# One mask matmul per unit, and the split transposed rows kept in DRAM for the second pass of self-attention

## The chip, the cores and the metric

The kernel runs on 1 core of one Trainium2 chip. The metric is device time in microseconds of one execution of the whole program: self-attention, cross-attention and a mixture of experts. A core has a matrix engine (TensorE, "PE" in the profile, with its weight loads as "PEld"), a vector engine (DVE), a scalar engine (ACT), GpSimd (POOL) and a sync engine (SP) which here only issues transfers; 16 DMA engines move data between DRAM and the on-chip memory SBUF. Each engine works through its own list of instructions in order, and engines wait for one another through semaphores.

## The reference

The change touches the first of three residual blocks:

```python
x = x + attn(layernorm(x))        # B=16, S=256, H=512
x = x + xattn(layernorm(x), ctx)  # untouched
x = x + experts(layernorm(x))     # untouched

# attn: 16 heads of 128, 4 key/value groups
q = (x @ w_q)                      # 512 -> 2048
k, v = split(x @ w_kv)             # 512 -> 4*128 each
scores = q @ k.T / sqrt(128);  scores[key > query] = -inf
probs = softmax(scores);  out = (probs @ v) @ w_dense
```

## The kernel before

Tokens are handled in *pairs*: two sequences, 512 tokens. There are 8 pairs (`PAIRS`), and they are run through twice (`HALVES`): the weights of all 16 heads don't fit in SBUF, so the first pass computes 8 heads, the second the other 8 and adds to the rows that the first pass stored. The loop variable `t` runs from 0 to 15; it is written as a loop over t = 0 to 6 (kind "plain"), t = 7 ("turn", where the next half's weights are loaded), t = 8 ("fresh"), a loop over t = 9 to 14 ("plain" again) and t = 15 ("last").

Precision is kept by splitting every float32 operand into a high part (an fp32r copy made by ACT) and a low part (the remainder, made by DVE). `product3` (L513) multiplies such pairs in three matmuls: high·high and the two mixed ones.

For each t the normalised rows are needed transposed and split, as `xT` (two tiles, 1 MB each). To make them for t+1, during pair t: SP loads the rows into `x_in` (L210); DVE computes `row_stats` in units 3 to 6 (L366), `mean_and_variance` in unit 7, `apply_norm` in units 9 to 12 (L376), with a power on POOL between them; PE transposes 16 blocks of 128 x 128 in units 14 and 15 (`xT_fill`, L531, eight in each); ACT and DVE split them (L336, L361). Both passes do this, from the same rows.

A pair then consists of 16 *units* u = 0 to 15, a unit being one head of one sequence. In unit u PE does, in this order: `scores(u)`; half a projection of a later query (`q_fill`, u up to 11); in odd units `values_product`, the product of probabilities and values for two earlier units; the transposes of the probabilities of unit u-1 (L591); in units 14 and 15 `xT_fill`; in units 12 to 15 a quarter of `dense`, the output projection. After unit 15 comes a tail: `k_fill` and `v_fill` of t+1, the rest of `dense`, two query projections and `scores(t+1, 0)`.

`scores` (L563) fills a PSUM bank in two blocks: queries 0 to 127 against 128 keys, and queries 128 to 255 against 256 keys. Each block is three split matmuls and then a bf16 matmul of the identity with a triangular block of -1e30 (L575, `causal`) which masks the diagonal 128 columns. The softmax of a unit follows on other engines: DVE takes two maxima (L404, L405), ACT two exponentials (L294, L296), DVE the inverse sums and the first third of the scaling (L412, L414), POOL the rest of the scaling (L260), then PE transposes the result (L591), ACT and DVE split that (L289, L361), and `values_product` uses it. On DVE, unit u is: maxima(u), the step of the normalisation if there is one, the inverse (u), in odd units the low parts of a query and of a context, and the low part of the transposed probabilities of u-1 (`pT_low_part`).

SP issues everything in one queue, in order: rows `x_in`, residual rows `acc`, and the store of `acc` at the end of a pair, each behind a wait.

Of the kernel before, what the change touches and what calls it, by code (L numbers as in the profile page):

```python
# [20 lines left out]
P = 128  # L21
BANK = 512
# [11 lines left out]

def attention_phase(nc, x_rows, w_q, w_kv, w_dense, x1_rows, TOKENS, HIDDEN, SEQ, HEADS, GROUPS):

# [17 lines left out]
    with ExitStack() as ctx:  # L54
# [6 lines left out]
        def sem(name):  # L61
            return ctx.enter_context(nc.semaphore("a_" + name))
# [48 lines left out]
        rstd_done = sem("rstd_done")  # L111
        xn_done = sem("xn_done")
        proj_filled = sem("proj_filled")
        proj_high = sem("proj_high")
# [24 lines left out]
        def heads_context(c, n):  # L139

            m, b = unit(2 * n)
            return c[:, m // HPG, m % HPG:m % HPG + 2, b * SEQ:(b + 1) * SEQ]

        def tokens(rows, pair):
# [46 lines left out]
        with nc.Block() as block:  # L191
            @block.sync
            def _(sp):
# [12 lines left out]
                def body(t, kind, half):  # L206
                    if kind != "last":
                        wait_alone(sp, xn_done, TB * (t + 1), (consts, 6))
                        nxt = 0 if kind == "turn" else t + 1 - half * PAIRS
                        sp.dma_start(x_in[:], tokens(x_rows, nxt)).then_inc(x_loaded, 16)  # L210
                    if kind == "fresh":
                        load_weights(1, DENSE)
                    if kind == "turn":
                        sp.wait_ge(proj_filled, FILLS * t + KT + G + 2)
                        load_weights(1, KV)
                    wait_alone(sp, stored, 16 * (t + 1), (consts, 6))
                    rows = x_rows if half == 0 else x1_rows
                    sp.dma_start(acc[:], tokens(rows, t - half * PAIRS)).then_inc(acc_loaded, 16)
                    if kind == "turn":
                        sp.wait_ge(proj_filled, FILLS * (t + 1))  # L220
                        load_weights(1, QUERY)
                    if kind != "last":
                        wait_alone(sp, d_added, G * TB * (t + 1) + 1, (consts, 6))
                        sp.dma_start(tokens(x1_rows, t - half * PAIRS), acc[:]).then_inc(stored, 16)
                    else:
                        for n in range(TB):
                            sp.wait_ge(d_added, TB * (G * t + G - 1) + n + 1 + 1)
                            sp.dma_start(tokens(x1_rows, t - half * PAIRS)[:, n, :], acc[:, n, :]).then_inc(stored, 16)
# [5 lines left out]
            def _(pool):  # L234
# [21 lines left out]
                def body(t, kind, half):  # L256
                    for u in range(UNITS):
                        s = u % 2
                        wait_alone(pool, rinv_done, UNITS * t + u + 1, (consts, 6))
                        nc.gpsimd.tensor_scalar(probs[:, s, P:3 * P], probs[:, s, P:3 * P], rinv[:, s, 1:2], None,  # L260
                                                ALU.mult).then_inc(probs_done, 1)
                        if u == TB + 3 and kind != "last":
                            norm_scale(t + 1)
# [4 lines left out]
            def _(act):  # L268
# [53 lines left out]
                def body(t, kind, half):  # L322
                    last = kind == "last"
                    for u in range(UNITS):
# [6 lines left out]
                        if u >= 1:  # L331
                            probs_transposed(t, u - 1)
                        if u in XT_STEPS and not last:
                            for j in range(*XT_STEPS[u]):
# [24 lines left out]
            def _(dve):  # L359
# [98 lines left out]
                def body(t, kind, half):  # L458
                    last = kind == "last"
                    for u in range(UNITS):  # L460
                        if u:
                            maxima(t, u)
                        if not last:

# [12 lines left out]
                        if u >= 1:  # L477
                            pT_low_part(t, u - 1)
                        if not last:
                            if u in XT_STEPS:  # L480
                                xT_low(t + 1, *XT_STEPS[u])
                        if kind == "turn" and u in SPLIT_AT_TURN[1]:
# [29 lines left out]
            def _(pe):  # L512
# [50 lines left out]
                def scores(t, u):  # L563
# [5 lines left out]
                    for qb in range(2):  # L569
                        c0, n = qb * P, (qb + 1) * P  # L570
                        q0 = b * SEQ + qb * P
                        product3(ps_s[s][:, c0:c0 + n], qT, (slice(None), m % 4, slice(q0, q0 + P)),
                                 kT, (slice(None), g, slice(b * SEQ, b * SEQ + n)), True, False)

                        ins = nc.tensor.matmul(ps_s[s][:, c0 + n - P:c0 + n], ident_b[:], causal[:], start=False, stop=True)  # L575
                    ins.then_inc(s_filled, 1)

# [58 lines left out]
                def body(t, kind, half):  # L636
                    last = kind == "last"
                    for u in range(UNITS):
# [7 lines left out]
                        if u >= 1:  # L646
                            transposes(t, u - 1)
                        if u in XT_STEPS and not last:
                            xT_fill(t + 1, *XT_STEPS[u])
                        if u == UNITS - 4:  # L650
                            pe.wait_ge(w_low, NCH * (half + 1))
# [3 lines left out]
                    if kind == "turn":  # L655
                        pe.wait_ge(w_low, NCH + KV[-1] + 1)
                    if not last:
                        k_fill(t + 1, 0)
# [1672 lines left out]
def decoder_layer(nc, x, context, mask, mask_cols, a_wq, a_wkv, a_wd, x_wq, x_bq, x_wk, x_bk, x_wv, x_bv,  # L2331
# [11 lines left out]

    attention_phase(nc, by_512(x), a_wq, a_wkv, a_wd, by_512(x1), B * S, H, S, HEADS, GROUPS)
    cross_attention_phase(nc, x1, context, mask, mask_cols, x_wq, x_bq, x_wk, x_bk, x_wv, x_bv, aux, rinv, x2)
# [45 lines left out]
```

## Time and profile before

| | |
|---|---|
| median of 3 runs (range) | 3019.73 us (3019.2 to 3022.58) |
| the profiled execution's own time | 3024.8 us |
| its span, first to last instruction | 3023.3 us |
| PE busy | 2648.8 us, 88% of the span |
| DVE busy | 1931.0 us (64%) |
| ACT busy | 1352.9 us (45%) |
| POOL busy | 1040.0 us (34%) |

Self-attention is the first part of the span, until 1392 us, when its last store is issued. In it the granted TensorE clock is full. A row of a timeline tells when an instruction started, how long it took, engine, source line, operation and operands, and in brackets how long the engine had been idle before it and for whom. Durations of matmuls include the time in the pipeline, so the distance between the *starts* of successive matmuls tells what one costs, not its duration.

### The profile page before, as it was taken

Reading aid. Unit: us, or ns where it says so; the run is one execution under the profiler, and the core shown is the slowest. Engines: PE = TensorE matmul, PEld = TensorE weight load, DVE = VectorE, ACT = ScalarE, POOL = GpSimd, SP = SyncE. Lnnn points to the kernel's source line nnn. Section 1 sums busy time; section 2 is a strip of 40 time slices with the busy share of each in tenths; the row PEclk is TensorE's granted clock in tenths of the full one; section 3 lists DMA queues with packets and bytes.
Section 4 is the critical chain, followed back from the end, with each engine's and each line's share of the span. In section 5 each row is a group of like instructions: output and inputs, shape, how many; then the busy total and the mean of one; then the engine's idle time right before and its main releaser. Section 6 shows DMA issues by size and latency. Waiting matters only on the chain. (4 is left out here: it accounts for less than half of the span.)

```text
span 3023.3 us, 49992 instructions
## 1 busy us (share of the span) xinstructions
PE 2648.8 (88%) x15042; PEld 1814.2 (60%) x15043; DVE 1931.0 (64%) x3971; ACT 1352.9 (45%) x2725; POOL 1040.0 (34%) x1209
## 2 busy tenths in 40 slices
PE   7999999999999999995788889888888434299997
PEld 6888888888888888884333333333333111166665
DVE  6555566656555666554888878888888278444443
ACT  4333444444333444432477766776666322022221
POOL 2111122211111222213355565566555346432322
PEclk9999999999999999997899999999999666599999
DMA  3110011122110111103666777777776264455554
GB/s 112 42 42 28 13 42 42 42 84 70 43 42 0 42 42 42 42 28 88 113 121 135 140 128 130 133 137 131 132 138 114 54 230 158 157 98 104 98 104 77
DMA packets 140545, 265.50 MB, mean 88 GB/s; under 512 B 39217, under 2 KB 42161, under 8 KB 138945
## 3 DMA queue, kind: packets, MB, share of 16 engines
q1 hardware_dynamic: 111376, 195.58, 29.1%
q0 software_dynamic: 24496, 60.72, 9.7%
q10 hardware_dynamic: 4608, 8.39, 0.8%
q8 instruction: 34, 0.56, 0.1%
q14 instruction: 31, 0.25, 0.0%
HBM read 139.43 MB, written 64.90 MB: 68 GB/s over the span
## 5 line engine op out<-in xcount | busy, mean ns | idle before, releaser
L1420 DVE TENSOR_REDUCE b_negmax<-b_ps_s 128x2 f32<-128x1024 f32 x512 | 616.8, 1221 | 117.6 <-PE b_ps_s L1563 114.2
L1292 ACT ACTIVATE b_probs<-b_ps_s 128x1024 f32<-128x1024 f32 x512 | 517.1, 1022 | 258.3 <-PE b_ps_s L1574 257.2
L260 POOL TENSOR_SCALAR probs<-probs,rinv 128x256 f32<-128x256 f32 x256 | 242.2, 946 | 1099.7 <-DVE rinv L412 1099.7
L294 ACT ACTIVATE probs<-ps_s,negmax 128x128 f32<-128x128 f32 x256 | 94.2, 368 | 480.6 <-DVE negmax L405 480.6
L1563 PE MATMUL b_ps_s<-b_stack 54*128 54x512 f32 x1024 | 228.8, 444 | 80.0 <-ACT b_probs L1292 50.1
L1574 PE MATMUL b_ps_s<-b_stack 56*128 56x512 f32 x1024 | 255.1, 496 | 49.4 <-DVE b_negmax L1420 30.8
L1574 PEld LDWEIGHTS b_ps_s<-b_stack 56*128 56x128 f32 x1024 | 97.9, 189 | 333.6 <-issue 183.9
L1585 PE MATMUL b_ps_o<-b_probs,b_v_stack 128*32 128x512 f32 x2048 | 283.6, 627 | 5.2 <-ACT b_probs L1292 5.2
L516 PE MATMUL ps_proj<-xT_h,wq_h 128*128 128x512 f32 x512 | 215.6, 421 | 0.0
L2181 POOL DMA_INDIRECT out<-e_y,e_place_int x71 | 110.8, 1560 | 277.1 <-DVE e_y L2244 174.7
L516 PE MATMUL ps_proj<-xT_h,wq_l 128*128 128x512 f32 x512 | 201.2, 393 | 0.0
L516 PE MATMUL ps_proj<-xT_l,wq_h 128*128 128x512 f32 x512 | 199.9, 390 | 0.0
L1563 PEld LDWEIGHTS b_ps_s<-b_stack 54*128 54x128 f32 x1024 | 101.2, 193 | 138.0 <-ACT b_probs L1292 79.5
L1171 POOL TENSOR_TENSOR b_out_tiles<-b_o_sb,b_out_tiles 128x512 f32<-128x512 f32 x64 | 82.5, 1290 | 263.1 <-DMA b_out_tiles<-row_sum_inverses 263.1
L516 PE MATMUL ps_s<-kT_h,qT_h 128*128 128x128 f32 (+1 forms) x512 | 164.3, 321 | 0.0
L516 PE MATMUL ps_d<-wd_h,cT_h 128*128 128x512 f32 x384 | 158.0, 412 | 1.4 <-DVE cT_l L361 1.4
L412 DVE RECIPROCAL rinv<-rowsum 128x2 f32<-128x2 f32 x256 | 42.3, 165 | 178.9 <-ACT probs L296 178.9
L2318 PE MATMUL e_ps_h<-c_w_h,e_xT_l 128*128 x284 | 152.5, 537 | 0.0
L516 PE MATMUL ps_d<-wd_h,cT_l 128*128 128x512 f32 x384 | 151.0, 393 | 0.0
L516 PE MATMUL ps_d<-wd_l,cT_h 128*128 128x512 f32 x384 | 150.6, 392 | 0.0
L361 DVE TENSOR_TENSOR pT_l<-ps_pT,pT_h 128x384 fp32r<-128x384 f32 x256 | 140.8, 550 | 2.6 <-ACT pT_h L289 2.6
L516 PE MATMUL ps_s<-kT_l,qT_h 128*128 128x128 f32 (+1 forms) x512 | 142.4, 278 | 0.0
(299 smaller groups left out, 6730.1 us busy)
## 6 DMA issues: line engine op xcount, KB each, us to landing
b_stack<-b_split SPq DMA_DIRECT2D x240, 128.0 KB
e_row<-rows_by_expert SPq DMA_DIRECT2D x71, 258.0 KB, 3.2
x_in<-in_x SPq DMA_DIRECT2D x16, 1024.0 KB, 7.5
b_out_tiles<-row_sum_inverses SPq DMA_DIRECT2D x64, 256.0 KB
x<-acc SPq DMA_DIRECT2D x15, 1024.0 KB, 5.1
b_stack<-b_late SPq DMA_DIRECT2D x96, 128.0 KB
acc<-in_x SPq DMA_DIRECT2D x8, 1024.0 KB, 6.0
acc<-x SPq DMA_DIRECT2D x8, 1024.0 KB, 5.7
```

The lines of the kernel that those rows point to most:

```text
L260: nc.gpsimd.tensor_scalar(probs[:, s, P:3 * P], probs[:, s, P:3 * P], rinv[:, s, 1:2], None, ALU.mult).then_inc(probs_done, 1)
L294: nc.scalar.activation(probs[:, s, 0:P], ps_s[s][:, 0:P], ACT.Exp, bias=negmax[:, s, 0:1], accum_out=rowsum[:, s, 0:1])
L361: return nc.vector.tensor_tensor(dst, ps, h.bitcast(F32), ALU.subtract)
L516: ins = nc.tensor.matmul(out, w[a][w_at], m[b][m_at], start=st, stop=en)
L1171: nc.gpsimd.tensor_tensor(r_b[:, q, :], o_sb[:, q, :], r_b[:, q, :], ALU.mult).then_inc(o_scaled, 1)
L1292: nc.scalar.activation(probs[:, k % 2, p, :, :], ps[:], ACT.Exp, scale=0.25).then_inc(e_done, 1)
L1420: nc.vector.tensor_reduce(negmax[:, k, p, :], ps[:], AX.X, ALU.max, negate=True).then_inc(m_reduced, 1)
L1563: ins = nc.tensor.matmul(ps[:, i, :], stack[rows, quad, 0, p, k * P:(k + 1) * P], stack[rows, quad, 1, p, :], start=True, stop=True)
L1574: ins = nc.tensor.matmul(ps[:, i, :], stack[rows, q, 1, p, k * P:(k + 1) * P], stack[rows, q, 0, p, :], start=True, stop=True)
L1585: ins = nc.tensor.matmul(ps_o[32 * h:32 * h + 32, :], v_stack[:, k, HQ * q + h, :], probs[:, k % 2, h // 2, h % 2, :], start=(k == 0), sto ...
L2181: nc.gpsimd.indirect_dma_start(out, bass.IndirectOffsetOnAxis(place_int[i][:], 0), y[i][:], None, compute_op=ALU.add).then_inc(y_out[i], 16)
L2318: ins = nc.tensor.matmul(ps_h[i][:], xT[a][:, i, j, :], w13[c][:, bass.ds(e, 1), j, :].rearrange("p o f -> p (o f)"), start=(m == 0), stop ...
```

## The change

There are two edits.

**The mask.** Instead of one bf16 matmul of 128 columns behind each of the two blocks, one matmul behind both adds the mask to the two diagonal blocks (columns 0 to 127 and 256 to 383) by strided and repeated access patterns. The flag that opens an accumulation is set only for the first block.

**The transposed rows.** A DRAM tensor `normalised_x_split` (16 MB) keeps `xT` of every pair. In the first pass SP stores both tiles; in the second pass, and for its first pair already in t = 7, SP loads them back once the last query projection of pair t has read the old ones. For these eight (t+1 = 8 to 15) the row load, the statistics, the normalisation, the 16 transposes and the splits are gone; what keeps the semaphore counts right are plain increments in unit 15. `k_fill` of t+1 now waits for the loads. The first pass is otherwise as it was.

```diff
+        def given(kind, half):
+            return kind == "turn" or half == 1 and kind != "last"
+        def made(kind, half):
+            return kind == "plain" and half == 0
 # SP
-                    if kind != "last":
+                    if kind == "plain" and half == 0:
                         wait_alone(sp, xn_done, TB * (t + 1), (consts, 6))
-                        nxt = 0 if kind == "turn" else t + 1 - half * PAIRS
-                        sp.dma_start(x_in[:], tokens(x_rows, nxt)).then_inc(x_loaded, 16)
+                        sp.dma_start(x_in[:], tokens(x_rows, t + 1)).then_inc(x_loaded, 16)
+                    if half == 0:
+                        wait_alone(sp, proj_low, FILLS * t + KT, (consts, 6))
+                        for i in range(2):
+                            sp.dma_start(xT_pairs[t, i], xT[i][:].bitcast(F32)).then_inc(xT_stored, 16)
...
                     if kind == "turn":
-                        sp.wait_ge(proj_filled, FILLS * (t + 1))
+                        sp.wait_ge(xT_stored, 32 * PAIRS)
+                    if given(kind, half):
+                        wait_alone(sp, proj_filled, FILLS * (t + 1), (consts, 6))
+                        for i in range(2):
+                            sp.dma_start(xT[i][:].bitcast(F32), xT_pairs[t + 1 - PAIRS, i]).then_inc(xT_loaded, 16)
+                    if kind == "turn":
                         load_weights(1, QUERY)
 # ACT (DVE and PE have the same pattern)
-                        if u in XT_STEPS and not last:
+                        if u == UNITS - 1 and given(kind, half):
+                            act.wait_ge(proj_filled, FILLS * (t + 1) + KT)
+                            act.sem_inc(proj_high, KT)
+                        if u in XT_STEPS and made(kind, half):
+                            if u == UNITS - 2:
+                                act.wait_ge(xT_stored, 32 * (t + 1))
 # DVE
-                        if not last:
+                        if made(kind, half):
                             if 3 <= u < 3 + TB:
                                 row_stats(t + 1, u - 3)
 # PE
                         product3(ps_s[s][:, c0:c0 + n], qT, (slice(None), m % 4, slice(q0, q0 + P)),
-                                 kT, (slice(None), g, slice(b * SEQ, b * SEQ + n)), True, False)
-                        ins = nc.tensor.matmul(ps_s[s][:, c0 + n - P:c0 + n], ident_b[:], causal[:], start=False, stop=True)
-                    ins.then_inc(s_filled, 1)
+                                 kT, (slice(None), g, slice(b * SEQ, b * SEQ + n)), qb == 0, False)
+                    diagonal = ps_s[s][:].rearrange("p (c k) -> p c k", c=BANK // P)[:, 0:3:2, :]
+                    nc.tensor.matmul(diagonal, ident_b[:], causal[:, None, :].to_broadcast([P, 2, P]),
+                                     start=False, stop=True).then_inc(s_filled, 1)
...
+                    if given(kind, half):
+                        pe.wait_ge(xT_loaded, 32 * (t + 2 - PAIRS))
                     if not last:
                         k_fill(t + 1, 0)
```

Where this puts the instructions can be seen in three places. On PE, unit 14 of a pair in the second pass's loop, before (`ps_s` is the bank of scores, `ps_pT` the transposed probabilities, `ps_proj<-ident,xn` the transposes of the normalised rows; the last two rows come a second time behind these, for the other bank, and then `dense`):

```order
L516 MATMUL ps_s<-kT_h,qT_l 128x128
L575 MATMUL ps_s<-causal,ident_b 128x128
L516 MATMUL ps_s<-kT_h,qT_h 128x256
L516 MATMUL ps_s<-kT_l,qT_h 128x256
L516 MATMUL ps_s<-kT_h,qT_l 128x256
L575 MATMUL ps_s<-causal,ident_b 128x128
L591 MATMUL ps_pT<-ident,probs 128x128 [waits a_probs_done,a_probs_done_first]
L591 MATMUL ps_pT<-ident,probs 128x128 x2
L527 ISA
L523 ISA [waits a_xn_done]
L531 MATMUL ps_proj<-ident,xn 128x128 [waits a_proj_low]
L531 MATMUL ps_proj<-ident,xn 128x128 x3
```

The same place on PE in the changed kernel, whose line numbers are higher:

```order
L543 MATMUL ps_s<-kT_h,qT_l 128x128
L543 MATMUL ps_s<-kT_h,qT_h 128x256
L543 MATMUL ps_s<-kT_l,qT_h 128x256
L543 MATMUL ps_s<-kT_h,qT_l 128x256
L603 MATMUL ps_s<-causal,ident_b 128x2x128
L619 MATMUL ps_pT<-ident,probs 128x128 [waits a_probs_done,a_probs_done_first]
L619 MATMUL ps_pT<-ident,probs 128x128 x2
L643 REGISTER_ALU
L543 MATMUL ps_d<-wd_h,cT_h 128x512 [waits a_d_added]
```

The first mask matmul is gone, the second covers both blocks, and the eight transposes of this unit (and eight in unit 15) have left PE. In the first pass the scores are the same as here, and the transposes stay.

On SP, the second pass's loop over t = 9 to 14, before:

```order
L210 ISA [waits a_xn_done,a_consts]
L210 DMA x_in<-in_x 128x4x512
L30 REGISTER_ALU
L218 ISA [waits a_stored,a_consts]
L218 DMA acc<-x 128x4x512
L30 ISA
L224 DMA x<-acc 128x4x512 [waits a_d_added,a_consts]
```

And the same loop on SP in the changed kernel:

```order
L231 ISA [waits a_stored,a_consts]
L231 DMA acc<-x 128x4x512
L237 ISA [waits a_proj_filled,a_consts]
L237 DMA xT_h<-normalised_x_split 128x2048
L237 ISA
L237 DMA xT_l<-normalised_x_split 128x2048
L30 ISA
L242 DMA x<-acc 128x4x512 [waits a_d_added,a_consts]
```

The 1 MB row load at the start of the pair is gone, and two loads of 1 MB stand behind the last query projection, in unit 11.

On PE, the end of unit 15 and the head of the tail in the changed kernel, second pass, where the wait for these loads stands (`a_xT_loaded`):

```order
L619 MATMUL ps_pT<-ident,probs 128x128 [waits a_probs_done,a_probs_done_first]
L619 MATMUL ps_pT<-ident,probs 128x128 x2
L689 ISA
L563 REGISTER_ALU [waits a_xT_loaded]
L550 REGISTER_ALU [waits a_proj_low]
L543 MATMUL ps_proj<-xT_h,wkv_h 128x512 [waits a_proj_low]
```

The first product of the tail is the first instruction that reads the loaded tiles.

## Rows read from the trace of the kernel before

**Rows 1.** Busy time by windows, 40 us of a second-pass pair; columns PE, PEld, DVE, ACT, POOL, granted clock, DMA share, GB/s

```profile
1065.00:1105.00 40.00, 40.00 (x251) 34.88 (x250) 29.09 (x83) 21.40 (x71) 11.64 (x13) 1.00 0.24 79
```

**Rows 2.** Waits in the first 1400 us; columns total us, times, longest us

```profile
DVE negmax L404 <- PE ps_s L575: 22.5, 15, 1.5
...
DVE stats L366 <- DMA x_in<-in_x: 18.4, 15, 7.0
...
PE ps_c L516 <- DVE pT_l L361: 4.6, 5, 1.8
...
PE ps_pT L591 <- POOL probs L260: 2.9, 8, 1.1
```

**Rows 3.** Timeline of PE, unit 11 of pair t = 12; columns start us, us

```profile
1098.11 0.27 PE L516 MATMUL ps_s<-kT_h,qT_l 128*128 128x128 f32 x1
...
1098.46 0.28 PE L516 MATMUL ps_s<-kT_l,qT_h 128*128 128x256 f32 x1
1098.58 0.28 PE L516 MATMUL ps_s<-kT_h,qT_l 128*128 128x256 f32 x1
1098.70 0.23 PE L575 MATMUL ps_s<-causal,ident_b 128*128 128x128 bf16 x1
...
1099.06 0.39 PE L516 MATMUL ps_proj<-xT_l,wq_h 128*128 128x512 f32 x1
1099.29 0.40 PE L516 MATMUL ps_proj<-xT_h,wq_l 128*128 128x512 f32 x1
```

**Rows 4.** Timeline of PE, first scores of units 14 and 15, pairs t = 11 and 15

```profile
1025.81 0.22 PE L516 MATMUL ps_s<-kT_h,qT_h 128*128 128x128 f32 x1
...
1030.60 0.22 PE L516 MATMUL ps_s<-kT_h,qT_h 128*128 128x128 f32 x1
...
1365.38 0.22 PE L516 MATMUL ps_s<-kT_h,qT_h 128*128 128x128 f32 x1
...
1369.32 0.22 PE L516 MATMUL ps_s<-kT_h,qT_h 128*128 128x128 f32 x1
```

**Rows 5.** Timeline of DVE, maxima of units 9 and 11, t = 7, and between

```profile
663.82 0.28 DVE L404 TENSOR_REDUCE negmax<-ps_s 128x1 f32<-128x128 f32 x1
...
665.42 0.17 DVE L412 RECIPROCAL rinv<-rowsum 128x2 f32<-128x2 f32 x1 [0.53 <-ACT probs L296]
...
670.05 0.28 DVE L404 TENSOR_REDUCE negmax<-ps_s 128x1 f32<-128x128 f32 x1
```

**Rows 6.** Timeline of DVE, maxima of units 1 and 11, pair t = 12

```profile
1068.77 0.29 DVE L404 TENSOR_REDUCE negmax<-ps_s 128x1 f32<-128x128 f32 x1 [1.50 <-PE ps_s L575]
...
1099.38 0.28 DVE L404 TENSOR_REDUCE negmax<-ps_s 128x1 f32<-128x128 f32 x1
```

**Rows 7.** Timeline of PE, transposes of the probabilities of unit 11, t = 12

```profile
1102.42 0.50 PE L591 MATMUL ps_pT<-ident,probs 128*128 128x128 f32 x3
```

**Rows 8.** Timeline of PE, first score of unit 0, pairs t = 9, 12, 13, 15

```profile
805.00 0.22 PE L516 MATMUL ps_s<-kT_h,qT_h 128*128 128x128 f32 x1
...
1060.02 0.22 PE L516 MATMUL ps_s<-kT_h,qT_h 128*128 128x128 f32 x1
...
1144.72 0.22 PE L516 MATMUL ps_s<-kT_h,qT_h 128*128 128x128 f32 x1
...
1314.87 0.22 PE L516 MATMUL ps_s<-kT_h,qT_h 128*128 128x128 f32 x1
```

**Rows 9.** Timeline of the DMA issues of SP, behind unit 11's query projection, t = 7

```profile
669.67 0.88 SPq L199 DMA_DIRECT2D wq_raw<-in_a_wq  x2
```

**Rows 10.** Timeline of PE, first matmul of the tail of t = 7

```profile
692.13 0.48 PE L516 MATMUL ps_proj<-xT_h,wkv_h 128*128 128x512 f32 x1
```

**Rows 11.** DMA issues, 668 to 690 us; columns KB each, median us to landing

```profile
wq_raw<-in_a_wq SPq DMA_DIRECT2D x2, 1024.0 KB, 7.1
```

**Rows 12.** DMA issues, whole trace, then 722 to 745 us (start of t = 8)

```profile
x_in<-in_x SPq DMA_DIRECT2D x16, 1024.0 KB, 7.5
...
x_in<-in_x SPq DMA_DIRECT2D x1, 1024.0 KB, 7.6
```

More of the change, by code:

```diff
@@ L32, in wait_alone, with attention_phase @@
     eng.wait_ge(sem, value)
-def attention_phase(nc, x_rows, w_q, w_kv, w_dense, x1_rows, TOKENS, HIDDEN, SEQ, HEADS, GROUPS):
+def attention_phase(nc, x_rows, w_q, w_kv, w_dense, xT_pairs, x1_rows, TOKENS, HIDDEN, SEQ, HEADS, GROUPS):
     D = P
@@ L112, in attention_phase @@
         xn_done = sem("xn_done")
+        xT_stored = sem("xT_stored")
+        xT_loaded = sem("xT_loaded")
         proj_filled = sem("proj_filled")
@@ L261, in body @@
                                                 ALU.mult).then_inc(probs_done, 1)
-                        if u == TB + 3 and kind != "last":
+                        if u == TB + 3 and made(kind, half):
                             norm_scale(t + 1)
@@ L478, in body @@
                             pT_low_part(t, u - 1)
-                        if not last:
-                            if u in XT_STEPS:
-                                xT_low(t + 1, *XT_STEPS[u])
+                        if made(kind, half) and u in XT_STEPS:
+                            if u == UNITS - 2:
+                                dve.wait_ge(xT_stored, 32 * (t + 1))
+                            xT_low(t + 1, *XT_STEPS[u])
+                        if u == UNITS - 1 and given(kind, half):
+                            dve.wait_ge(proj_high, FILLS * (t + 1) + KT)
+                            dve.sem_inc(proj_low, KT)
                         if kind == "turn" and u in SPLIT_AT_TURN[1]:
@@ L647, in body @@
                             transposes(t, u - 1)
-                        if u in XT_STEPS and not last:
+                        if u in XT_STEPS and made(kind, half):
                             xT_fill(t + 1, *XT_STEPS[u])
+                        if u == UNITS - 1 and given(kind, half):
+                            pe.wait_ge(proj_low, FILLS * (t + 1))
+                            pe.sem_inc(proj_filled, KT)
                         if u == UNITS - 4:
@@ L2342, in by_512 @@
         return t.rearrange("(g b) s h -> g (b s) h", b=BANK // S)
-    attention_phase(nc, by_512(x), a_wq, a_wkv, a_wd, by_512(x1), B * S, H, S, HEADS, GROUPS)
+    xT_pairs = nc.dram_tensor("normalised_x_split", [B * S // BANK, 2, P, H // P, BANK], F32, kind="Internal").ap()
+    attention_phase(nc, by_512(x), a_wq, a_wkv, a_wd, xT_pairs, by_512(x1), B * S, H, S, HEADS, GROUPS)
     cross_attention_phase(nc, x1, context, mask, mask_cols, x_wq, x_bq, x_wk, x_bk, x_wv, x_bv, aux, rinv, x2)
```

## The prediction, made before the changed kernel ran

> **What bounds the kernel now.** I read the busy time by windows first, then the list of waits, then timelines of single pairs. The window shows PE busy for all of its 40 us, at full clock, and DVE for 29 [rows 1]: by busy time the phase is PE's, and everything taken off PE is gained. The waits say it more sharply. In the first 1400 us PE waits 4.6 us for DVE and 2.9 us for POOL. But DVE, which takes 256 maxima, waits for PE's scores only 15 times, once per pair, in unit 1 [rows 2, 6]. An engine that never waits for PE in units 2 to 12 is as slow as PE there. So I looked at its pace.
>
> DVE's maxima of units 9 and 11 start 6.23 us apart [rows 5]. Within, DVE waits for ACT's exponentials even behind a normalisation step (0.53 us idle before the inverse [rows 5]): that step lies in ACT's shadow, and taking it away only makes the idle longer. DVE and PE meet in the softmax of unit 11: its transposes stand behind the scores of unit 12 without a query projection between, so there PE meets DVE's result. In t = 12 the maxima of unit 1 start at 1068.77, those of unit 11 at 1099.38 (30.61 us), and the transposes start 3.04 us later, behind the inverse and POOL's scaling [rows 6, 7]. The row of these transposes has no wait in brackets: PE's own work took the same 33.65 us, so the two are level. PE can get faster, but those 33.65 us stay, a floor that DVE, ACT and POOL set from unit 1 to the transposes in unit 12. Outside (units 13, 14, 15, the tail, units 0 and 1) DVE waits for PE.
>
> **The mask.** A matmul's price is the distance of starts. From the last 128-column split matmul to the second 256-column one are 0.35 us, with the mask and one 256-column matmul between; the unmasked steps would be 0.12 + 0.12 (the step from 1098.46 to 1098.58), so the mask costs 0.11 to 0.12. From the last 256-column one to the second projection matmul are 0.48 us, of which 0.12 and 0.23 are theirs: 0.13 [rows 3]. A mask of 128 columns thus costs as much as a 256-column matmul (0.12). So I take it that a mask of 256 columns costs the same 0.12 to 0.13, and one of two vanishes: 0.12 us per unit. The bounds: the longer stream adds what half a 256-column matmul does, 0.06, and only 0.06 is saved; or the changed weights between 128- and 256-column groups cost nothing extra, and 0.13 is.
>
> The rule against this is in the Trainium skill, "TensorE: Matmul & The Clock Gate", section "Step-by-step: what each phase is for": the array takes in one column per cycle, so a stream costs its columns alone. By it two masks of 128 and one of 256 cost the same and this edit gives 0. Its figure for 128 columns is 55.6 ns; the trace disagrees, with 110 to 130 ns for these, so I follow the trace and keep the rule as a rival.
>
> There are 256 units, but the gain counts only where PE is the later one. Scores(2) to scores(12), 11 of 16, lie inside the floor. If PE gets ahead by 11 x 0.12 = 1.3 us there, it waits 1.3 us for POOL before the transposes of unit 11, or earlier for DVE before a `values_product`. Five per pair are left (units 13, 14, 15, 0, 1): 80 x 0.12 = **9.6 us** (4.8 at 0.06, 10.4 at 0.13).
>
> **The transposes.** Unit 14 takes 4.79 us in t = 11, with eight transposes, and 3.94 us in t = 15, which makes none [rows 4]: 0.85 us for eight, 1.70 for 16. Units 14 and 15 lie outside the floor. Nothing else comes to bind: t = 15 runs the same DVE adds and softmax, and PE had no wait in its 3.94. Eight pairs (t = 7 to 14) lose them: 8 x 1.70 = **13.6 us** (12.8 if the transposes of unit 15 were partly hidden, 14.4 if ACT's and DVE's splits held something back).
>
> **Statistics, normalisation, splits** on DVE, ACT and POOL: 0, since DVE's pace does not come from them. But the row load is waited for, 18.4 us in 15 times, one of them 7.0 at the start [rows 2], and that wait, in unit 3, is longer than ACT's shadow in some pairs and lengthens the floor. The six pairs t = 9 to 14 take (1314.87 - 805.00) / 6 = 84.98 us on average; t = 12 takes 84.70 [rows 8]. Without a row load all should be like t = 12: 6 x 0.28 = 1.7, and some 0.3 for t = 7 and 8: **2.0 us**. In the first pass the wait stays, and scores(1) now end 0.12 earlier than the unmoved landing of the rows: -0.4 us for seven pairs.
>
> **The loads.** In t = 7 SP issues two loads of 1 MB behind unit 11's query projection, at 669.67, exactly where the new loads go; they land 7.1 us after issue [rows 9, 11]. The first reader of `xT`, the tail's first matmul, starts at 692.13 [rows 10], 22.5 us after. Less the 1.7 us of transposes that leaves 20.8: the loads are hidden with over 12 us to spare. Nothing is queued behind the wait for `proj_filled` on SP but the store at the pair's end. In t = 7 the 2 MB of query weights move behind the new 2 MB; at the same rate they land by about 14 to 15 us after issue, and their first reader on ACT stands in unit 15. Cost 0.
>
> **The stores.** In the first pass 2 MB go out behind the row load and before `acc`. Does that delay the rows, which DVE waits for? At t = 8 two 1 MB weight loads are issued right behind the rows, and the rows land after 7.6 us [rows 12], against a median of 7.5 over all 16. What is queued behind does not delay. `acc` comes later by up to 6 us and is not read before unit 12. The tiles are overwritten in unit 14, over 50 us later. Cost 0, at most the 0.5 us by which loads differ, in seven pairs: 3.5.
>
> **The sum.** 9.6 + 13.6 + 2.0 - 0.4 = 24.8 us off the profiled execution's 3024.8, which is 3000.0. Its median is 5.1 us lower, and nothing here depends on that: 3019.7 - 24.8 = **2994.9**, say 2995. Edges from the bounds: 4.8 + 12.8 + 0 - 0.4 - 3.5 = 13.7 off (3006); 10.4 + 14.4 + 2.5 = 27.3 off (2992). The later phases stay as they are, at the same clock.
>
> **The rivals.**
> *The floor does not hold.* If DVE's chain follows PE (its lag behind the scores is nearly constant within a pair, as a follower's would be), all 256 masks count: 256 x 0.12 = 30.7, and with 13.6 + 2.0 that is 46 off: 2973. Against it: DVE is idle in units 2 to 12 only for ACT, never for scores. 8%.
>
> *The merged mask saves nothing.* Its columns cost in full, or the strided output and the repeated input cost as much as a second matmul. Then 13.6 + 1.6 = 15.2 off: 3004.5. For it stands the column count; against it the 0.12 us for 128 columns. 13%. The rule of the Trainium skill named above gives this case.
>
> *The loads come too late.* One mechanism: `k_fill` of eight tails waits for `xT_loaded`. It starts to cost when 2 MB take over 20.8 us, and turns the whole into a loss when they take 3.1 us more (24.8 / 8), 24 us, against 7.1 measured; at 28 us it would be 8 x 7.2 - 24.8 = +33, or 3053. For it: in no trace were fp32r tiles written by 8 KB rows during units 11 to 15. Against it: three times the time. 4%.
>
> That the change does not do what it says can be left out for the transposes, which leave the list of PE.
>
> **Chances.** Forecast 72%, floor broken 8%, mask free of gain 13%, loads late 4%, and 3% for something that I don't see. The range of 80% goes from 2984 to 3007: it takes in the forecast's own 2992 to 3006 and the useless mask, with some room below for a floor that gives way in part, and leaves out the broken floor and the late loads. A measurement here tells 0.2%, 6 us, from nothing. Faster by more: the first three cases, 92%. Within: 4%, for a useless mask together with a small cost of the stores. Slower: 4%.
>
> **What would show it.** PE should have 256 mask matmuls of 256 columns and 128 fewer transposes. Units 14 and 15 of t = 7 to 14 should be shorter by 0.85 + 0.12 each; t = 9 to 14 should take 84.7 - 1.7 - 0.6 = 82.4 us each, all alike, and pairs of the first pass 84.2 to 84.9 instead of 84.8 to 85.5. PE's waits for POOL before the probabilities' transposes and for DVE before `values_product` should grow from 7.5 us to about 7.5 + 16 x 1.2 = 27 us: that is where the other 11 masks go. From the maxima of unit 1 to the transposes of unit 11 it should still be 33.6 us. If that stretch is 32.3, the floor was none. If the distance of starts across the merged mask is 0.18 or more, the mask term is too large. A wait of PE for a transfer ahead of the tail would show the late loads, and waits for rows in the first pass over 1.4 us a cost of the stores.

## The result and the profile after

The changed kernel takes 3005.2 us in the median of five runs (3002.5 to 3010.2), the kernel before 3019.7 (five runs, 3016.9 to 3025.1). The ratio is 0.9948, with a 95% interval from 0.9932 to 0.9964: 14.5 us less (10.9 to 20.5). The forecast was 24.8 less. The direction is right, the time lies inside the range, and some ten microseconds of the gain are missing. The measured 3005.2 is nearer to 3004.5, the figure of the rival in which the merged mask saves nothing, than to the forecast's 2994.9. The time alone would speak for that rival; it takes the traces and the experiments to tell them apart.

The page of the changed kernel (busy time, share of the span, instructions) shows that the work did go:

```profile
span 3008.7 us, 49088 instructions
...
PE 2619.4 (87%) x14658; PEld 1775.2 (59%) x14659; DVE 1879.3 (62%) x3843; ACT 1331.9 (44%) x2693; POOL 1029.5 (34%) x1193
```

The groups of PE by line and form in the first 1400 us (busy us, mean ns, idle before) have one mask per unit, 256 columns wide, and half of the 256 transposes of the normalised rows:

```profile
L603 PE MATMUL ps_s<-causal,ident_b 128*128 128x256 bf16 x256 | 72.9, 285 | 0.0
...
L558 PE MATMUL ps_proj<-ident,xn 128*128 128x128 f32 x128 | 18.4, 292 | 14.2 <-DVE xn L399 13.3 <-DVE xT_l L384 0.8
```

**Where the time came from.** The first scores of unit 0 in pairs t = 1, 7, 9 and 15, on PE's timeline (start us, us); the answer to [rows 8]:

```profile
117.79 0.22 PE L543 MATMUL ps_s<-kT_h,qT_h 128*128 128x128 f32 x1
...
630.18 0.22 PE L543 MATMUL ps_s<-kT_h,qT_h 128*128 128x128 f32 x1
...
802.59 0.22 PE L543 MATMUL ps_s<-kT_h,qT_h 128*128 128x128 f32 x1
...
1298.22 0.22 PE L543 MATMUL ps_s<-kT_h,qT_h 128*128 128x128 f32 x1
```

The six pairs t = 9 to 14 take 1298.22 - 802.59 = 495.63 us, 82.6 each and all alike within 0.03; before they took 509.87 [rows 8]. That is 14.24 less. Pairs t = 7 and 8 give 4.4 more. The pairs of the first pass, however, became slower: t = 1 to 6 take 630.18 - 117.79 = 512.39 us, 85.40 each. Before they began at 118.00 and 628.21, 510.21 us or 85.04 each. Up to the start of t = 15 the changed kernel is 1314.87 - 1298.22 = 16.65 us ahead. The cross-attention begins 18.6 us earlier (its first row on DVE starts at 1376.59 instead of 1395.18).

From there to the end this one execution took 4.0 us more than the one of before. Nothing there was changed. Over eleven profiled executions of this case's kernels that stretch took between 1617.1 and 1636.7 us, so a difference of 4 between two of them tells nothing. I compare the attention by its landmarks and the whole by the medians.

**What is waited for.** The list of waits in the first 1400 us (total us, times, longest us), to be read beside [rows 2]:

```profile
DVE rinv L435 <- ACT probs L314: 217.6, 250, 1.5
...
DVE negmax L427 <- PE ps_s L603: 22.2, 15, 1.5
DVE stats L389 <- DMA x_in<-in_x: 15.9, 7, 6.7
...
PEld ps_c L543 <- issue: 12.2, 32, 1.0
PEld ps_pT L619 <- issue: 10.2, 22, 0.6
...
PE ps_c L543 <- DVE pT_l L384: 8.5, 11, 2.4
...
PE ps_pT L619 <- POOL probs L278: 5.9, 17, 0.4
```

The row of the kernel before that belongs to the first:

```profile
DVE rinv L412 <- ACT probs L296: 178.9, 242, 1.2
```

Three things stand in it. PE's two rows grew from 7.5 to 14.4 us, and the idle time of the weight loads for which the profile names nobody (the "issue" rows) from 4.6 to 22.4: PE now meets the softmax chain more often. DVE waits for rows only 7 times instead of 15, but still 15.9 us, instead of 18.4: without the 6.7 at the start, 1.5 us per wait where there were 0.8. And DVE, which lost half of its normalisation work, waits 39 us longer for ACT's exponentials: most of the work taken off it became idle time. No wait of PE for the loaded `xT` is in the list.

### The profile page after: what moved, and what is told of

Its sections match the earlier page's. It is cut to its first block and busy times, and to the rows that moved or that the text cites. A ratio compares the mean times of both kernels' runs of the same rounds, so it can differ in the third digit from the quotient of the medians.

```text
span 3008.7 us, 49088 instructions
## 1 busy us (share of the span) xinstructions
PE 2619.4 (87%) x14658; PEld 1775.2 (59%) x14659; DVE 1879.3 (62%) x3843; ACT 1331.9 (44%) x2693; POOL 1029.5 (34%) x1193
## 5 line engine op out<-in xcount | busy, mean ns | idle before, releaser
L543 PE MATMUL ps_s<-kT_h,qT_h 128*128 128x128 f32 (+1 forms) x512 | 156.7, 306 | 0.0
L543 PE MATMUL ps_s<-kT_h,qT_l 128*128 128x128 f32 (+1 forms) x512 | 142.2, 278 | 0.0
```

The source lines that it names most:

```text
L543: ins = nc.tensor.matmul(out, w[a][w_at], m[b][m_at], start=st, stop=en)
```

## The experiments

Each pair's start stands for the pace of the attention. "Second-pass pairs" are t = 9 to 14.

**The mask alone.** The kernel before, with this edit:

```diff
-    ... kT, (...), True, False)
-    ins = nc.tensor.matmul(ps_s[s][:, c0 + n - P:c0 + n], ident_b[:], causal[:], start=False, stop=True)
-  ins.then_inc(s_filled, 1)
+    ... kT, (...), qb == 0, False)
+  diagonal = ps_s[s][:].rearrange("p (c k) -> p c k", c=BANK // P)[:, 0:3:2, :]
+  nc.tensor.matmul(diagonal, ident_b[:], causal[:, None, :].to_broadcast([P, 2, P]), ...)
```

> The kernel before with the merged mask alone. In the changed kernel the merged mask saves 0.06 us per unit, not 0.12. Theory (floor): DVE, ACT and POOL set 33.6 us from the maxima of unit 1 to the transposes of unit 11, so only 5 of 16 units count: 80 x 0.063 = 5 us, less about 1 us because the row loads, still waited for in both passes, now come later than the earlier scores: 3.5 to 5 us faster than before, pairs of 84.5 to 85.3 us, unit 12 growing from 4.0-4.4 to 4.5. Rival (no floor): all 256 units count, 16 us faster, pairs of 83.8 us.

Measured: a ratio to before of 0.9985 (0.9963 to 1.0008), which the clock alone can't tell from 1. The trace can. PE in unit 12 of t = 12 (start us, us, wait in brackets), up to the first scores of unit 13:

```profile
1098.33 0.30 PE L516 MATMUL ps_s<-kT_h,qT_h 128*128 128x128 f32 x1
...
1099.73 0.52 PE L592 MATMUL ps_pT<-ident,probs 128*128 128x128 f32 x3 [0.35 <-POOL probs L260]
...
1102.86 0.22 PE L516 MATMUL ps_s<-kT_h,qT_h 128*128 128x128 f32 x1
```

t = 15 starts at 1311.29, 3.6 us earlier than before, the cross-attention 4.0. Unit 12 takes 4.53 us, where it took 4.00: PE comes early and waits for POOL's scaled probabilities. The even units take 2.54 us instead of 2.60, so the merged mask does save something in each. So the floor is real, and the 4 us are what is left of the 16 that 256 units would give.

**The stored rows alone.** The changed kernel, with the mask of before:

```diff
-    ... kT, (...), qb == 0, False)
-  diagonal = ...
-  nc.tensor.matmul(diagonal, ident_b[:], causal[:, None, :].to_broadcast([P, 2, P]), ...)
+    ... kT, (...), True, False)
+    ins = nc.tensor.matmul(ps_s[s][:, c0 + n - P:c0 + n], ident_b[:], causal[:], start=False, stop=True)
```

> The changed kernel with the two masks of before, so the DRAM edit alone. Theory: transposes of eight pairs 8 x 1.75 = 14 us, waits for rows gone in the second pass 2 us, and 2 to 3.5 us lost in the first pass to the stores behind the row load: 12 to 14 us faster than before; second-pass pairs 82.9 to 83.0 us, first-pass pairs 85.0 to 85.4. Rival (mask counts in full, no floor): the DRAM edit would be worth only the difference to 16 us, some 0 to 3 us.

Measured: 0.9956 (0.9939 to 0.9973). t = 15 starts at 1303.48, 11.4 us ahead of before, the cross-attention 13.0 ahead. Second-pass pairs take 83.0, those of the first pass 85.7 to 85.9 (85.0 to 85.4 were expected), against 85.04: storing makes each of them 0.7 slower. Together with the mask alone, 11.4 + 3.6 = 15.0, this gives nine tenths of the 16.65. The merged mask is worth a little more beside this edit: in the six second-pass pairs it saves 498.08 - 495.63 = 2.45 us with the row loads gone, and 1.75 alone.

**No mask at all.** The changed kernel, with the causal mask left out of the self-attention's scores:

```diff
+    ins = product3(ps_s[s][:, c0:c0 + n], ..., True, True)
+  ins.then_inc(s_filled, 1)
-  diagonal = ...
-  nc.tensor.matmul(diagonal, ident_b[:], ...)
```

> The changed kernel without any mask matmul; the causal mask is left out of the computation. PE loses another 0.12 us per unit. Theory (floor): only the five units per pair outside it count, 80 x 0.12 = 9.6 us against the changed kernel, second-pass pairs from 82.6 to 82.0 us, the stretch from unit 1's maxima to unit 11's transposes still 33.5 us and unit 12 growing to 5.8. Rival (no floor): 256 x 0.12 = 31 us, pairs of 80.7 us.

Measured, in one run: 2994.9 us. PE at the transposes of unit 11, in unit 12 of t = 12:

```profile
1085.51 0.52 PE L616 MATMUL ps_pT<-ident,probs 128*128 128x128 f32 x3 [0.48 <-POOL probs L278]
```

Second-pass pairs take (1289.49 - 797.73) / 6 = 81.96 us, 0.65 less than with the merged mask: that is 5 units of 0.13. If all 16 counted, it would be 80.5 to 80.7. A unit is 2.41 instead of 2.54, but units 7, 9 and 11 of t = 12 grow from 3.57, 3.58 and 3.64 to 3.80 or 3.81. Unit 12 stays at 4.52, where 5.8 was expected: the lead is lost earlier, before `values_product`, and not all at once in unit 12. The merged mask costs its 0.13, and only five of 16 are paid for by the clock.

This is also where DVE's own pace can be read, since PE is fastest here. Its maxima of units 9 and 11 of t = 12 (DVE, start us, us):

```profile
1076.29 0.28 DVE L427 TENSOR_REDUCE negmax<-ps_s 128x1 f32<-128x128 f32 x1
...
1082.49 0.28 DVE L427 TENSOR_REDUCE negmax<-ps_s 128x1 f32<-128x128 f32 x1
```

They are 6.2 us apart, and PE's units 8 to 11 take 2.41 + 3.81 or 3.80, as much. In the changed kernel the same maxima are 6.21 us apart (1083.30 to 1089.51), though PE's units there take 2.54 + 3.57; in the kernel before 6.25 (1093.13 to 1099.38), where PE's take 2.60 + 3.64 = 6.24. So DVE's pace stays when PE gets faster, and before the change PE was the slower of the two by 0.03 us in two units.

**The stores later.** The changed kernel, the two stores moved from before `acc`'s fetch to behind it:

```diff
-  if half == 0:
-      wait_alone(sp, proj_low, FILLS * t + KT, (consts, 6))
-      ... the two stores
   ... acc's fetch
+  if half == 0:
+      wait_alone(sp, proj_filled, FILLS * t + 13, (consts, 6))
+      ... the two stores
```

> The changed kernel with the first pass's stores of the transposed tiles issued in unit 6, behind the load of acc, instead of right behind the row load. Theory (stores delay the rows): the rows land 7.5 us after issue again instead of 8.1, the interval of unit 5 in pairs 1 to 6 falls from 4.2-4.5 to about 3.9, and these pairs from 85.4 to 84.9 us: 3 to 4 us off the whole attention. Rival (the rows are late only because DVE now asks 0.25 us earlier): landing stays at 8.1 us and the pairs at 85.4.

Here the views of transfers and of DVE belong together. The changed kernel, first: the issues on SP in t = 2, without the second store (start us, us), the landing of these transfers (KB each, us from issue), and DVE's first statistics:

```profile
211.36 0.39 SPq L219 DMA_DIRECT2D x_in<-in_x  x1
212.07 1.08 SPq L223 DMA_DIRECT2D normalised_x_split<-xT_h  x1
```

```profile
x_in<-in_x SPq DMA_DIRECT2D x1, 1024.0 KB, 8.1
normalised_x_split<-xT_h SPq DMA_DIRECT2D x1, 1024.0 KB, 9.9
normalised_x_split<-xT_l SPq DMA_DIRECT2D x1, 1024.0 KB, 11.1
acc<-in_x SPq DMA_DIRECT2D x1, 1024.0 KB, 11.0
```

```profile
219.47 0.69 DVE L389 BATCH_NORM_STATS2 stats<-x_in 128x6 f32<-128x512 f32 x1 [1.52 <-DMA x_in<-in_x]
```

And with the stores behind:

```profile
x_in<-in_x SPq DMA_DIRECT2D x1, 1024.0 KB, 7.4
acc<-in_x SPq DMA_DIRECT2D x1, 1024.0 KB, 5.5
normalised_x_split<-xT_h SPq DMA_DIRECT2D x1, 1024.0 KB, 3.9
normalised_x_split<-xT_l SPq DMA_DIRECT2D x1, 1024.0 KB, 5.8
```

```profile
218.61 0.69 DVE L389 BATCH_NORM_STATS2 stats<-x_in 128x6 f32<-128x512 f32 x1 [0.83 <-DMA x_in<-in_x]
```

The rows land after 7.4 us instead of 8.1, and DVE waits 0.83 instead of 1.52. Pairs t = 1 to 6 take 84.80 on average instead of 85.40: 3.6 us in six pairs. One run gave 3004.0 us, but its t = 15 starts at 1295.51, 2.7 ahead of the changed kernel. t = 2 is not alone: the rows of t = 1 to 6 land after 7.9 to 8.2 us in the changed kernel, 6.9 to 7.9 with the stores later, and 7.0 to 7.9 in the kernel before. Stores issued 0.7 us behind this load do slow it.

**The rows early.** The changed kernel, with the row load of pair t + 2 issued in unit 12 of pair t, when `x_in` has long been read (and so behind the stores of that pair). The load for pair 1 stands ahead of the loop, which the cut does not show, and the pass of t = 6 is written out without a load:

```diff
-  if kind == "plain" and half == 0:
-      wait_alone(sp, xn_done, TB * (t + 1), (consts, 6))
-      sp.dma_start(x_in[:], tokens(x_rows, t + 1)).then_inc(x_loaded, 16)
   ... acc's fetch
+  if kind == "plain" and half == 0 and more:
+      wait_alone(sp, xn_done, TB * (t + 2), (consts, 6))
+      sp.dma_start(x_in[:], tokens(x_rows, t + 2)).then_inc(x_loaded, 16)
```

> The changed kernel with the first pass's row load issued one pair ahead, in unit 12, as soon as its buffer is free. Theory: DVE's wait for rows falls from 15.9 to 6.7 us (the start alone), pairs 1 to 6 from 85.4 to 84.4 us, 82.6 of the second pass and 1.75 of transposes; 6 us off attention. Rival (the stores slow something else in the first pass): these pairs stay above 84.8.

Measured, in one run: 3002.6 us. Pairs t = 1 to 6 take 84.39 to 84.45, 1.0 less than in the changed kernel, t = 15 starts at 1292.92 (5.3 earlier). No first-pass pair waits for rows any more: only the 6.8 us at the start are left. With the wait gone the first-pass pairs are all alike, as those of the second pass were. The rows themselves land after 5.2 us here (the median of the page). At their old place they are issued 1.0 us behind the 1 MB store of `acc`, before and after the change (in t = 2 of the changed kernel 211.36 against 210.38), and took 7.5 us before it: that place was a poor one even without the new stores.

**The rows early and the dense step split.** On top of it, the first half of `dense(t, 0, 0)`'s products (six of twelve) goes before the transposes of unit 11, so that PE has work while POOL scales:

```diff
+  if u == UNITS - 4:
+      pe.wait_ge(w_low, NCH * (half + 1))
+      dense(t, 0, 0, 0)
   ... transposes of the probabilities
-      dense(t, 0, 0)
+      dense(t, 0, 0, 1)
```

> The changed kernel with both remedies together: the first pass's row load issued one pair ahead, in unit 12, and half of the dense product of unit 12 put ahead of the transposes of unit 11. Theory: first-pass pairs lose the wait for rows (-1.0 us each, 6 us in all) and all pairs the wait of 0.5 us in unit 12 (-8 us in all): attention ends 14 us earlier than in the changed kernel, cross-attention starts at 1362 to 1364 us instead of 1376.6, and the whole is 28 to 31 us (0.9 to 1.0%) faster than before. Rival (the wait only moves to the next result of DVE): no more than the 6 us of the row loads.

Measured: 2996.5 us, a ratio to before of 0.9904 (0.9882 to 0.9926). By medians that is 27.2 us off, where 28 to 31 were expected. Its interval doesn't touch that of the changed kernel in the first measurement (0.9932 to 0.9964), but overlaps that of the changed kernel measured beside it (0.9916 to 0.9962, below). What speaks for it is the trace: its t = 15 starts 12.9 us ahead of the changed kernel's first trace, and 13.7 ahead of the second. PE in unit 12 of t = 12, its scores, the transposes and the scores of unit 13:

```profile
1079.56 0.30 PE L553 MATMUL ps_s<-kT_h,qT_h 128*128 128x128 f32 x1
...
1081.85 0.49 PE L629 MATMUL ps_pT<-ident,probs 128*128 128x128 f32 x3
...
1083.56 0.22 PE L553 MATMUL ps_s<-kT_h,qT_h 128*128 128x128 f32 x1
```

The bracket at the transposes is gone, unit 12 is 4.00 again, and second-pass pairs take (1285.37 - 792.19) / 6 = 82.20, 0.41 less. Unit 13 grew from 4.97 to 5.03, which I hadn't counted. The cross-attention starts 12.0 us ahead of the changed kernel's, where 14 were expected.

**The blocks swapped.** The changed kernel, with the 256-key block of the scores computed first:

```diff
-  for qb in range(2):
+  for qb in (1, 0):
```

> The changed kernel with the 256-key block of scores computed before the 128-key block. In the changed kernel two steps across the change from 128 to 256 columns take 0.28 us instead of 0.23. Theory A (a stream of 256 columns behind one of 128 costs 0.05 more, whatever the matmul): the 0.05 moves to the mask behind the 128-column block, even units stay at 2.54 us and pairs at 82.6. Theory B (0.05 belongs to the first matmul of each block): also 2.54, with the 0.05 at the first 128-column matmul. Rival (it was the price of a stationary tile loaded behind a short stream, and 128 columns last hide it no worse): 2.49 us and 82.35.

First the masks' neighbourhood as the changed kernel has it, unit 2 of t = 12 (PE, start us, us), the answer to [rows 3]:

```profile
1060.74 0.28 PE L543 MATMUL ps_s<-kT_h,qT_l 128*128 128x128 f32 x1
...
1061.02 0.28 PE L543 MATMUL ps_s<-kT_l,qT_h 128*128 128x256 f32 x1
1061.14 0.28 PE L543 MATMUL ps_s<-kT_h,qT_l 128*128 128x256 f32 x1
1061.26 0.28 PE L603 MATMUL ps_s<-causal,ident_b 128*128 128x256 bf16 x1
1061.29 0.48 PE L543 MATMUL ps_proj<-xT_h,wq_h 128*128 128x512 f32 x1
1061.61 0.39 PE L543 MATMUL ps_proj<-xT_l,wq_h 128*128 128x512 f32 x1
```

The merged mask: 1061.14 to 1061.61 is 0.47, less 0.12 and 0.23 leaves 0.12, as forecast. But where the first mask was, from the last 128-column product to the second 256-column one, there are 0.28 us, not 0.12 + 0.12: before, with the mask between them, it was 0.35 [rows 3]. So the mask that went had cost 0.07, because 0.05 of its time had covered a step from 128 to 256 columns that is now bare. The kernel without any mask confirms it: the same distance is 0.28 there too (in unit 1 of t = 12, 1051.32 to 1051.60). Then the swapped blocks:

```profile
1063.75 0.28 PE L543 MATMUL ps_s<-kT_h,qT_l 128*128 128x256 f32 x1
1063.86 0.22 PE L543 MATMUL ps_s<-kT_h,qT_h 128*128 128x128 f32 x1
1063.92 0.27 PE L543 MATMUL ps_s<-kT_l,qT_h 128*128 128x128 f32 x1
1064.03 0.28 PE L543 MATMUL ps_s<-kT_h,qT_l 128*128 128x128 f32 x1
1064.15 0.29 PE L603 MATMUL ps_s<-causal,ident_b 128*128 128x256 bf16 x1
...
1064.51 0.39 PE L543 MATMUL ps_proj<-xT_l,wq_h 128*128 128x512 f32 x1
```

From the last 256-column product to the second 128-column one there are 0.17 us (1063.75 to 1063.92), where the other order has 0.28 for its two steps. Not all of these 0.11 are gained: the block that now comes first starts with wider products, and in unit 2 of t = 12 its second product starts 0.45 us behind the first of the transposes ahead of it (1057.17 to 1057.62) instead of 0.38 (1060.24 to 1060.62). A unit takes 2.48 or 2.49 instead of 2.54, and second-pass pairs 82.42 instead of 82.61, near the rival's 82.35: the extra 0.05 belongs to this order of widths. The reason that the rival gave, a stationary tile loaded behind a short stream, isn't shown by this. One run gave 3007.6 us; the 0.2 per pair can't be seen in a single time.

**The changed kernel again**, on the chip of the three versions above (rows early, dense step split, blocks swapped):

> The changed kernel once more, on the chip of the others, to compare with. Theory: attention is the same to 0.5 us in each execution (cross-attention starts at 1376.6), and what differs from one execution to the next, up to 10 us, is cross-attention. So 16 to 18 us faster than before on one chip. Rival: the stores and loads of the transposed rows leave something behind that costs the later phases 4 us each time, as in the first trace: 14.5 us.

Measured: 3006.3 us, 0.9939 (0.9916 to 0.9962). Second-pass pairs take 82.6 to 82.7, first-pass pairs 85.3 to 85.6, t = 15 starts at 1299.08. By medians that is 17.4 us less than the kernel before on this chip, as expected. Up to t = 15 the attention repeats within a microsecond; its last pair took 1.6 us longer, so that the cross-attention starts at 1379.07 and not at the 1376.6 that were expected. The stretch after it took 1627.8 us, 4.3 less than in the first trace of the same kernel, which speaks against the rival. This interval's lower end (25.4 us off) would just allow the forecast's 24.8; the first one's doesn't.

**All three together:** rows early, dense step split, blocks swapped.

> The early row load and the split dense step, and now also the 256-key block of the scores first. Theory (the floor from the maxima of unit 1 to the transposes of unit 11 holds; the change from 128- to 256-column products costs 0.05 us in a unit): only the 5 units outside the floor count, 5 x 0.055 = 0.2 to 0.3 us a pair, so second-pass pairs of 81.9 to 82.0 us (82.2 without the swap), first-pass pairs of 83.7 (83.95), unit 12 grown to 4.4 to 4.6 (4.0), and about 4 us less than the version without the swap: near 2993 us, a ratio to the kernel before of about 0.989. Rival (with the split step the floor has given way and PE sets the pace alone): all 16 units count, 0.9 us a pair: pairs of 81.3, unit 12 still 4.0, some 14 us less, near 2982. Second rival (the two edits meet at unit 12 and nothing more is gained): pairs of 82.2, 2996 to 2997.

Measured: 2985.8 us (six runs from 2982.1 to 2997.1), a ratio of 0.9894 (0.9862 to 0.9926). The time is nearer to the rival's 2982 than to the theory's 2993, but the pairs decide: those of the second pass take 82.02, those of the first 83.75 to 83.78, as the theory had it, and not 81.3. By the clock, on another chip, this can't be told from the version without the swap; by the pairs it is 0.18 or 0.19 us faster in each. The theory was wrong on the place: unit 12 is 3.87, not 4.4 to 4.6. The floor shows in units 7, 9 and 11 of t = 12, at 3.70 to 3.74 instead of 3.58 to 3.66. PE's weight load for `values_product` in unit 9 of t = 12, and the step of DVE ahead of it:

```profile
1070.01 0.19 PEld L553 LDWEIGHTS ps_c<-pT_h,v_h 128*128 128x128 f32 x1 [0.33 <-issue]
```

```profile
1069.33 0.55 DVE L394 TENSOR_TENSOR pT_l<-ps_pT,pT_h 128x384 fp32r<-128x384 f32 x1
```

`values_product` needs `pT_l`, which DVE ends at 1069.88; the weights are read from 1070.01. Two units take 2.48 + 3.74 = 6.22 us (units 10 and 11), against DVE's pace of 6.21. The floor is no single meeting in unit 12: it is the pace of the softmax chain, and it is met at the first point where PE's lead is used up. That DVE and ACT together set this pace, and not one of them, is argued from DVE's waits for the exponentials; no run changed either.

## Why the prediction was right in direction and too large

**The floor: right, and the most useful step.** In t = 12 the maxima of unit 1 and the transposes of unit 11 (DVE and PE timelines of the changed kernel), to be read beside [rows 6, 7]:

```profile
1059.05 0.29 DVE L427 TENSOR_REDUCE negmax<-ps_s 128x1 f32<-128x128 f32 x1 [1.48 <-PE ps_s L603]
```

```profile
1091.11 0.30 PE L543 MATMUL ps_s<-kT_h,qT_h 128*128 128x128 f32 x1
...
1092.53 0.52 PE L619 MATMUL ps_pT<-ident,probs 128*128 128x128 f32 x3 [0.35 <-POOL probs L278]
```

The stretch is 33.48 us, against 33.65 before and "still 33.6" in the forecast. "The two are level" was nearly right: PE had been the slower one by 0.17 us in this stretch, and that much of the mask's saving counted inside it. PE gained 0.6 in ten of these units and waited nearly all of it in unit 12: from its scores to its transposes 1.42 us, before 0.92. The rival "the floor does not hold" is refuted three times: by the mask alone (4 us, not 16), by no mask (81.96 us a pair), and by all three edits.

**The mask: the mechanism right, the term mis-sized.** The step "it costs 0.11 to 0.12, and one of two vanishes: 0.12 us per unit" took the steps beside the mask from a place where nothing changed width. The units say what was saved. Ten units of t = 12 before, from the first scores of unit 2 to those of unit 12:

```profile
1070.26 0.30 PE L516 MATMUL ps_s<-kT_h,qT_h 128*128 128x128 f32 x1
...
1101.50 0.30 PE L516 MATMUL ps_s<-kT_h,qT_h 128*128 128x128 f32 x1
```

That is 31.24 us. After, from 1060.48 to 1091.11, it is 30.63: 0.061 per unit, and 80 x 0.061 = 4.9 us instead of 9.6. The distances beside the mask say the same: 0.07 us for the mask that went, and nothing more for the wider one that stayed. The forecast named this value as its bound (0.06), for a reason that is refuted: the longer stream does not cost more (the merged mask takes 0.12). The rival "saves nothing" is refuted too, by the 0.06 us of each unit and the 3.6 to 4.0 us of the mask alone. The rule behind it, in the Trainium skill ("TensorE: Matmul & The Clock Gate", section "Step-by-step: what each phase is for"), by which a stream costs its columns alone, does not fit the steps of this trace: 0.12 us for the merged mask of 256 columns, and 0.13 for one of 128 before it.

**The transposes: right.** Unit 14 takes 1104.52 - 1100.60 = 3.92 us instead of 4.79 [rows 4], unit 15 with the tail 28.47 instead of 29.41. Less 0.06 us of mask in each, that is 0.81 + 0.88 = 1.69 us a pair, against 1.70.

**Statistics, normalisation, splits at 0: right.** In the changed kernel the maxima of units 9 and 11 are 6.21 us apart in t = 12, where this work is gone, and 6.21 in t = 5, where it is still done. DVE's waits for the exponentials grew by 39 us instead.

**The row waits of the second pass: right.** Six pairs gave 14.24; less 6 x (1.69 + 5 x 0.061) that leaves 2.3 where 1.7 were forecast. The stored rows alone tell the two apart: 509.87 - 498.08 - 6 x 1.69 = 1.65 us of row waits. The other 0.6, 0.1 in each pair, is what the mask saves inside the floor's stretch. t = 7 and 8 gave 0.4 as against 0.3.

**The stores: the step that failed.** "What is queued behind does not delay", it said, from weight loads issued behind the rows, 7.6 against 7.5 us [rows 12]. Those did not delay, as far as one transfer tells, though the first of them was issued only 0.5 us behind the rows. But the stores are issued 0.7 us behind the rows, and with them the rows land after 8.1 us (7.4 when the stores come later). Moving them gave back 3.6 us, the size of the bound of 3.5 that the forecast had put to this and then left out of its sum. Whether it is their direction, their target or how soon the second follows the first that makes stores do what loads did not was not tried. So the pairs of the first pass, forecast at 84.2 to 84.9 us, take 85.25 to 85.53. A second, smaller part was forecast: DVE is ready earlier by the mask's 0.06 or 0.12, so the wait grows (0.4 us).

**The loads: right.** On the turn both 1 MB loads are issued behind unit 11's projection and land within 7 us. The transfers issued from 668 to 690 us (KB each, median us to landing), beside [rows 11]:

```profile
wq_raw<-in_a_wq SPq DMA_DIRECT2D x2, 1024.0 KB, 12.0
xT_h<-normalised_x_split SPq DMA_DIRECT2D x1, 1024.0 KB, 4.8
xT_l<-normalised_x_split SPq DMA_DIRECT2D x1, 1024.0 KB, 6.9
```

The weights behind them land after 12.0 us instead of 7.1 and nobody waits for it.

**The sign that was off.** PE's two rows of waits were to grow from 7.5 to about 27 us. They grew to 14.4. With a mask of 0.061 in 11 of 16 units it would have been about 18; the rest of what PE lost stands in the "issue" rows of the weight loads, which the forecast had not named.

**The balance** up to the start of t = 15: masks 15 x 5 x 0.061 = 4.6 and 0.6 inside the floor, transposes 8 x 1.69 = 13.5, row waits 2.1, less 3.6 for the stores and 0.4 for the earlier DVE, is 16.8; measured 16.65. Of the 10.3 us between forecast and median the mask explains 4.1 (9.6 less 4.9 and 0.6) and the stores 3.6. The rest, 2.6 us, lies within what the later phases vary from one execution to the next, and I can't attribute it. The last pair's stretch to the cross-attention is one of these: it took 78.4 us here and 80.3 before, and 78.3 to 80.5 over the other runs.

## What to carry to other kernels

Read an instruction's price where it stands, and ask what it covered: a neighbour that seems free beside it may cost once it is gone, and the way to size that is a place in the trace that already has the new neighbourhood, or a one-line run. Before counting a saving on the busiest engine, find the stretch in which another chain is level with it and count only the instructions outside; an engine that never waits for PE inside a loop is the sign, and the pace that it keeps in a version where PE is faster is the proof. Look at what is issued close before and behind a transfer that something waits for: here its landing was late with the stores close behind it, and early only with nothing near it. Where its buffer is free earlier, issue it there, as the two best versions here do.

## What the runs showed of the hardware

- After fp32r products of 128 columns, the next two steps into products of 256 columns take 0.28 us together, where one step at 128 columns (0.11) and one at 256 (0.12) make 0.23. From 256 to 128 columns two steps take 0.17, but over a whole unit the swapped order saves only the 0.05. A bf16 mask between the two widths had covered the 0.05: with it the distance was 0.35, where 0.28 + 0.12 would be 0.40.
- An identity product in bf16 between fp32r products costs 0.12 to 0.13 us behind products of 256 columns, whether it has 128 or 256 columns itself. Between the products of 128 and those of 256 columns the one of 128 cost 0.07.
- Two stores of 1 MB issued 0.7 us behind a load of 1 MB bring its landing from 7.4 to 8.1 us, and that of the load behind them from 5.5 to 11.0. Issued later, with nothing else in flight, they land after 3.9 and 5.8 us. The same load of rows, issued with nothing near it, lands after 5.2 us.
